# Moving the product dt·u to VectorE, and reordering loads and steps, in a fused two-layer graph kernel

## What is computed

```python
# layer 0
h  = relu(adj @ x @ gcn_w + gcn_b);  h = layernorm(h) * ln_g + ln_b
xc, z = split(h @ w_in)                        # 256 + 256 columns
u  = silu(causal_conv4(xc) + conv_b)
dbc = u @ w_xp                                 # 8 columns of dt, 16 of B, 16 of C
dt = softplus(dbc[:, :8] @ w_dt + b_dt)
state[t] = exp(dt[t] * A) * state[t-1] + dt[t] * B[t] * u[t]      # 256 x 16, along all 4096 rows
y  = (state[t] @ C[t] + u * D_skip) * silu(z)
x1 = layernorm(x + y @ w_out)
# layer 1
o1 = mlp3((2 + eps1) * (adj @ x1));  o2 = mlp3((2 + eps2) * (adj @ x2))
out = layernorm(x1 + concat(o1, o2) @ Wm.T + bm)
```

## Time and profile before

| | |
|---|---|
| median of 3 runs | 820.49 us (820.03 to 822.79) |
| the profiled execution | 821.7 us |
| its span, first to last instruction | 819.9 us |
| TensorE busy | 805.8 us (98%) |
| VectorE busy | 599.7 us (73%) |
| ScalarE busy | 377.9 us (46%) |
| GpSimd busy | 659.7 us (80%) |
| DMA | 227.6 MB, mean 278 GB/s |

### The profile page before, as it was taken

One profiled execution on the slowest core, in us unless ns is written; L12 is line 12 of the kernel. 1 busy time (PEld: TensorE's weight loads), 2 busy tenths in 40 slices (PEclk: granted clock), 3 DMA queues, 4 the chain that ended last, 5 costly groups with the idle time before them and its releaser, 6 DMA issues.

```text
span 819.9 us, 7302 instructions
## 1 busy us (share of the span) xinstructions
PE 805.8 (98%) x2078; PEld 365.8 (45%) x2078; DVE 599.7 (73%) x800; ACT 377.9 (46%) x615; POOL 659.7 (80%) x318
## 2 busy tenths in 40 slices
PE   8899999999999999999999999999999999999996
PEld 3344444444444444444444444444444454444453
DVE  0034898799868986898799879887988889882135
ACT  0154465357535653475347534652466445231234
POOL 2005999999999899899999999889998999970036
PEclk9999999999999999999999999999999999999999
DMA  8979767675766899899778976789867896887602
GB/s 336 385 270 368 267 242 250 231 251 201 271 202 201 333 349 355 343 352 361 245 249 320 379 278 213 254 291 384 295 235 272 327 329 245 297 306 261 254 26 78
DMA packets 63388, 227.59 MB, mean 278 GB/s; under 512 B 7394, under 2 KB 8052, under 8 KB 44916
## 3 DMA queue, kind: packets, MB, share of 16 engines
q1 hardware_dynamic: 24660, 156.33, 50.9%
q10 hardware_dynamic: 38688, 70.80, 26.4%
HBM read 224.48 MB, written 2.62 MB: 277 GB/s over the span
## 4 chain that ended last, share of the span: by engine, by line
PE 95%; DMA 4%; ACT 1%; DVE 0%; issue 0%; DVEq 0%
PE p_x L486 51%; PE p_x L509 16%; PE p_two L509 11%; DMA x_s<-x_tiles 3%; PE p_m L582 2%; PE p_dA L677 2%; PE p_m L598 2%; PE p_two L572 1%; PE p_m L565 1%; DMA ring<-adj_blocks 1%; PE p_m L602 1%; PE p_m L536 1%; PE p_m L542 1%; PE p_h L677 1%; PE p_m L594 1%; PE p_two L552 1%
## 5 line engine op out<-in xcount | busy, mean ns | idle before, releaser
L486 PE MATMUL p_x<-ring,x_s 128*128 128x512 f32 x1024 | 459.2, 597 | 4.2 <-DMA x_s<-x_tiles 4.2
L1125 POOL TENSOR_TENSOR y<-y,prod 128x1024 f32<-128x1024 f32 x127 | 299.4, 2357 | 26.6 <-DVE prod L942 25.9
L486 PEld LDWEIGHTS p_x<-ring,x_s 128*128 128x128 f32 x1024 | 193.8, 191 | 252.1 <-issue 242.5
L1116 POOL TENSOR_TENSOR bh<-spread,dtu 128x1024 f32<-128x1024 f32 x128 | 302.1, 2360 | 2.1 <-DMA spread<-bc_rows 2.0
L933 DVE TENSOR_TENSOR_SCAN p_h<-p_dA,state,bh 128x512 f32<-128x512 f32 x224 | 276.2, 1279 | 25.3 <-ACT p_dA L687 11.3
L687 ACT ACTIVATE p_dA<-dt,A 128x512 f32<-128x512 f32 x256 | 170.8, 686 | 113.0 <-DVE p_h L933 109.9
L942 DVE TENSOR_TENSOR prod<-p_h,spread_C 128x1024 f32<-128x1024 f32 x128 | 155.3, 1213 | 0.0
L509 PE MATMUL p_x<-ring,x 128*128 128x512 f32 x304 | 137.2, 593 | 0.0
L509 PE MATMUL p_two<-ring,x 128*128 128x512 f32 x208 | 94.5, 593 | 0.5 <-DVE dt L992 0.5
L509 PEld LDWEIGHTS p_x<-ring,x 128*128 128x128 f32 x304 | 57.4, 190 | 72.6 <-issue 72.6
L415 POOL TENSOR_SCALAR dtu<-prod,mv,rstd 128x128 f32<-128x128 f32 x26 | 20.3, 794 | 64.0 <-ACT rstd L920 64.0
(11 more groups left out here) (125 smaller groups left out, 579.9 us busy)
## 6 DMA issues: line engine op xcount, KB each, us to landing
ring<-adj_blocks SPq DMA_DIRECT2D x143, 1024.0 KB, 7.2
spread<-bc_rows ACTq DMA_DIRECT2D x128, 256.0 KB, 5.1
spread_C<-bc_rows ACTq DMA_DIRECT2D x128, 256.0 KB, 5.7
ring<-adj_blocks SPq DMA_DIRECT2D x8, 256.0 KB, 5.8
x_s<-x_tiles SPq DMA_DIRECT2D x8, 256.0 KB, 7.4
x_s<-x_tiles ACTq DMA_DIRECT2D x7, 256.0 KB, 7.5
out_tiles<-dtu SPq DMA_DIRECT2D x7, 256.0 KB, 2.0
pack<-pack_w ACTq DMA_DIRECT2D x1, 1026.5 KB, 11.2
```

The source lines that it names most:

```text
L486: return pe.matmul(bank[:, :], tiles[:, JT * m + jt, :], ring[:, i % RING, jt, :], start=opens, stop=closes)
L1116: pool.tensor_tensor(bh[:, i % 3, :, :], both(spread[:, i % SLOTS, :]), dtu[:, c % 2, :, :], ALU.mult).then_inc(s_bmul, 1)
L1125: pool.tensor_tensor(y[:, c % 2, :, :], y[:, c % 2, :, :], prod[:, i % 2, :, :], ALU.add).then_inc(s_acc, 1)
```

## The change

- "dt_sum" on VectorE writes max(v, 0) + ln(...) back into the banks (`s_dtsum`), ScalarE copies them to `dt_` (new step "dt_copy" at unit 11, ahead of "y_init", `s_dt`), VectorE multiplies the banks by u (new step "dtu" at unit 11, place 1, `s_dtu`, two instructions). The product on GpSimd is gone. TensorE's waits for the banks are on `s_dtu` in place of `s_dt`.
- In the fill, ScalarE takes softplus before it issues the first two broadcast rows of B.
- x1 is issued without a wait, x2 to x7 behind earlier landings than before, and the pack behind x7.
- The MLP steps of chunks 1 to 6 come half a unit later, the second of chunk 7 one unit sooner.
- The last "out" comes behind one block of `AFTER_BLOCKS`.
- VectorE no longer negates the means; ScalarE negates rstd. The state is not copied in the last chunk.

```diff
-        return [(c - 1, (24, 26, 28, 30))]
-    return [(6, (6, 9, 12, 15)), (7, (24, 26, 28, 30))]
+        return [(c - 1, (25, 27, 29, 31))]
+    return [(6, (6, 9, 12, 15)), (7, (22, 24, 26, 28))]
...
                         if unit > origin(chunk) and chunk + 1 < NC:
-                            pe.wait_ge(s_dt, G * (chunk + 1) + 1)
+                            pe.wait_ge(s_dtu, G * (chunk + 1) + 1)
...
                 elif name == "z":
-                    pe.wait_ge(s_dt, G * (n + 1))
+                    pe.wait_ge(s_dtu, G * (n + 1))
...
                     if n < 6:
-                        pe.wait_ge(s_dt, G * (n + 3))
+                        pe.wait_ge(s_dtu, G * (n + 3))
...
             block_part(AFTER_AT, 0, JT)
-            block_part(AFTER_AT + 1, 0, JT)
             step("out", NC - 1)
-            for i in range(AFTER_AT + 2, TAIL_AT):
+            for i in range(AFTER_AT + 1, TAIL_AT):
...
+                elif name == "dt_copy":
+                    for q, (g, bank) in enumerate(((1, p_two), (0, p_m))):
+                        act.wait_ge(s_dtsum, G * n + q + 1)
+                        act.activation(dt_[:, b, g, :], bank[:, :], ACT.Copy).then_inc(s_dt, 1)
...
+                    act.activation(nrstd[:, :], rstd[:, b, :], ACT.Copy, scale=-1.0).then_inc(s_rv, 1)
+                    act.wait_ge(s_rv, 3 * n + 3)
                     for t in range(JT):
-                        last = act.activation(shift[:, t:t + 1], nmean[:, t:t + 1], ACT.Copy, scale=rstd[:, b, t:t + 1])
+                        last = act.activation(shift[:, t:t + 1], mv[:, b, t, 0:1], ACT.Copy, scale=nrstd[:, t:t + 1])
...
                     put(o + 6, "softplus", c + 1)
+                    put(o + 7, "dt_copy", c + 1)
                     put(o + 7, "y_init", c + 1)
...
-                if k < 4:
-                    act.wait_ge(s_tile[(0, 0, 3, 7)[k]], 32 if k == 1 else 16)
-                else:
-                    act.wait_ge(*filled(k - 2))
+                if k == 2:
+                    act.wait_ge(s_tile[1], 32)
+                elif k in (3, 4):
+                    act.wait_ge(s_tile[3 * k - 7], 16)
+                elif k > 4:
+                    act.wait_ge(*filled(k - 3))
                 act.dma_start(x_s[:, JT * k:JT * (k + 1), :], x_d[k]).then_inc(s_xs[k], 16)
-                if k == 6:
-                    act.dma_start(pack[:, :], pack_d).then_inc(s_pack, 16)
+            act.dma_start(pack[:, :], pack_d).then_inc(s_pack, 16)
...
-                if name == "rows":
+                if name == "softplus":
                     for i in range(AHEAD):
                         spread_row(i)
...
-                dve.tensor_copy(state[:, unit, :], p_h[:, :, T - 1]).then_inc(s_state, 1)
+                if c < NC - 1:
+                    dve.tensor_copy(state[:, unit, :], p_h[:, :, T - 1]).then_inc(s_state, 1)
...
                     for g, bank in ((1, p_two), (0, p_m)):
-                        dve.scalar_tensor_tensor(out=dt_[:, b, g, :], in0=bank[:, :], scalar=0.0, in1=dt_[:, b, g, :],
-                                                 op0=ALU.max, op1=ALU.add).then_inc(s_dt, 1)
+                        dve.scalar_tensor_tensor(out=bank[:, :], in0=bank[:, :], scalar=0.0, in1=dt_[:, b, g, :],
+                                                 op0=ALU.max, op1=ALU.add).then_inc(s_dtsum, 1)
+                elif name == "dtu":
+
+                    dve.wait_ge(s_u, G * (n + 1))
+                    for q, (g, bank) in enumerate(((1, p_two), (0, p_m))):
+                        dve.wait_ge(s_dt, G * n + q + 1)
+                        dve.tensor_tensor(dtu[:, b, g, :], bank[:, :], u[:, g, :], ALU.mult).then_inc(s_dtu, 1)
...
                     put(o + 7, 0, "dt_sum", c + 1)
+                    put(o + 7, 1, "dtu", c + 1)
...
-                if name == "dtu":
-                    pool.wait_ge(s_dt, G * (n + 1))
-                    pool.wait_ge(s_u, G * (n + 1))
-                    pool.tensor_tensor(dtu[:, b, :, :], dt_[:, b, :, :], u[:, :, :], ALU.mult).then_inc(s_dtu, 1)
...
```

More of the change, by code:

```diff
@@ L297, in two_layer_graph_kernel @@
         rstd = sb("rstd", [P, 4, JT])
-        nmean = sb("nmean", [P, JT])
+        nrstd = sb("nrstd", [P, JT])
         shift = sb("shift", [P, JT])
@@ L365, in two_layer_graph_kernel @@
         s_dbcp, s_xpart, s_xsum, s_dbc = (sem(n) for n in ("s_dbcp", "s_xpart", "s_xsum", "s_dbc"))
[L366 to L370, removed]
+        s_dtp, s_abs, s_sp, s_dtsum, s_dt, s_dtu, s_yinit = (sem(n) for n in (
+            "s_dtp", "s_abs", "s_sp", "s_dtsum", "s_dt", "s_dtu", "s_yinit"))
+        s_yg, s_o, s_r, s_stats, s_rv, s_shift, s_x1 = (sem(n) for n in (
+            "s_yg", "s_o", "s_r", "s_stats", "s_rv", "s_shift", "s_x1"))
         s_mm2, s_mr2, s_res0, s_res1, s_two_add = (sem(n) for n in ("s_mm2", "s_mr2", "s_res0", "s_res1", "s_two_add"))
@@ L762, in step @@
                 elif name == "silu":
-                    wait(act, s_dtu, n)
+                    wait(act, s_dtu, G * n)
                     wait(act, s_yinit, G * n)
@@ L865, in _ @@
             take_x(0)
-            for name in ("gcn", "cen", "var", "in_x", "silu", "log_exp", "x_part", "rows", "softplus", "y_init"):
+            for name in ("gcn", "cen", "var", "in_x", "silu", "log_exp", "x_part", "rows", "softplus", "dt_copy", "y_init"):
                 step(name, 0)
@@ L928, in scans @@
                 wait(dve, s_cmul, i)
-                wait(dve, s_state, i)
+                wait(dve, s_state, min(i, S * (NC - 1)))
                 for g in range(G):
@@ L999, in step @@
                     statistics(r4, s_stats, n)
-                    aggregate(s_stats, b).then_inc(s_aggr, 1)
-                    dve.wait_ge(s_aggr, n + 1)
-                    dve.tensor_scalar(nmean[:, :], mv[:, b, :, 0], -1.0, None, ALU.mult).then_inc(s_stats, 1)
+                    aggregate(s_stats, b).then_inc(s_stats, 1)
                 elif name == "mlp3":
@@ L1051, in _ @@
             dve.wait_ge(s_two_add, 1)
-            for name in ("var", "taps0", "taps1", "x_sum", "dt_sum"):
+            for name in ("var", "taps0", "taps1", "x_sum", "dt_sum", "dtu"):
                 step(name, 0)
@@ L1076, in _ @@
             add_sum(SUM_OF[AFTER_AT])
-            add_sum(SUM_OF[AFTER_AT + 1])
             step("out", NC - 1)
-            for no in range(SUM_OF[AFTER_AT + 2], SUM_OF[TAIL_AT]):
+            for no in range(SUM_OF[AFTER_AT + 1], SUM_OF[TAIL_AT]):
                 add_sum(no)
@@ L1112, in times_B @@
                 if unit == 0:
-                    pool.wait_ge(s_dtu, c + 1)
+                    pool.wait_ge(s_dtu, G * (c + 1))
                 wait(pool, s_scan, G * (i - 2))
@@ L1128, in step @@
             def step(name, n):
-                b = n % 2
-                if name == "dtu":
-                    pool.wait_ge(s_dt, G * (n + 1))
-                    pool.wait_ge(s_u, G * (n + 1))
-                    pool.tensor_tensor(dtu[:, b, :, :], dt_[:, b, :, :], u[:, :, :], ALU.mult).then_inc(s_dtu, 1)
-                elif name == "gate_y":
+                if name == "gate_y":
                     pool.wait_ge(s_acc, S * (n + 1))
                     pool.wait_ge(s_gate, n + 1)
-                    pool.tensor_tensor(y[:, b, :, :], y[:, b, :, :], gate[:, :, :], ALU.mult).then_inc(s_yg, 1)
+                    pool.tensor_tensor(y[:, n % 2, :, :], y[:, n % 2, :, :], gate[:, :, :], ALU.mult).then_inc(s_yg, 1)
                 elif name == "resid":
@@ L1163, in _ @@
             pool.tensor_copy(wx3[:, :, ROW_B + S:ROW_B + 2 * S], w_xp[:, :, R + S:R + 2 * S]).then_inc(s_wx3, 1)
-            step("dtu", 0)
             for i in range(AHEAD):
@@ L1174, in _ @@
                         step("gate_y", c - 1)
-                    if c + 1 < NC and unit == origin(c) + 8:
-                        step("dtu", c + 1)
                     if i + AHEAD < S * NC:
```

4 lines of the change are left out of this document (2 added, 2 removed).

## The result

| | before | changed |
|---|---|---|
| median, timed together | 820.64 us (819.10 to 823.83, 6 runs) | 823.49 us (822.72 to 825.55, 6 runs) |
| the profiled execution | 821.7 us | 822.72 us |
| its span | 819.9 us | 820.9 us |
| mean granted clock of TensorE in it | 0.998 | 0.995 |

A forecast was written before the change was run, and what follows sets the result against it. TensorE, busy 98% of the span, was taken as the bound, so only its gaps could pay. Ramp -2.5 us and chunk 2's stall +2.5 us summed to 0.0: 820.5 us on the median, range 817.7 to 823.6.

The forecast's parts named there:

- ramp: At the start, x tiles issued ahead of weights close two DMA gaps: -2.5 us, bounds -0.8 and -3.7.
- line 536: The matmul after the ramp that first needs the pack; a sign of the forecast was its start near 37.3 us.
- (b): Rival: scan work falls behind TensorE through ScalarE's queue and VectorE's unit 11, stalling chunks 3 and 5; 824.3 us, chance 0.10.
- (d): Rival: at the ramp the first gap closes but block 7 lands where x7 did; ramp 0, 823.0 us, chance 0.10.
- The stall: In chunk 2, p_two's opening waits for VectorE's product with u: +2.5 us, bounds +1.3 and +3.8.
- Block 1: At the ramp, with x1 there, its first load starts near 11.1 us, 1.49 us sooner.
- The wait of block 2: At the ramp, x tiles moved forward delay this weight block on full DMAs, so it binds near 15.3 us.
- Block 7: At the ramp, the last to land, at 32.8 us, first load 32.85; wrong if landing before 31 or after 34.
- The pack: The 1 MB transfer issued after x7 lands at about 33 to 34 us, hidden with over 2 us of cover.
- Softplus first: In the fill, ScalarE's softplus starts about 4 us sooner, ahead of B's broadcasts; worth 0 us.
- (a): Rival: the ramp gives much (-3.7 us) and chunk 2's stall is short (+1.3 us); 817.5 us, chance 0.17.
- (c): Rival: the pack lands late, at 38 us, and holds line 536, costing 1.6 us; 822.1 us, chance 0.05.

The follow-up runs named there:

- e12: The kernel before the change, with no edit, traced a second time; 819.51 us in one execution.
- e2: The kernel before with only the dt change (sums in the banks, ScalarE's copy, VectorE's product with u); 825.20 us against 820.67, ratio 1.0057.
- e3: The kernel before with all edits of the change except the x order with the pack and the dt change; 820.44 us against 820.67, ratio 1.0001.
- e7: The kernel before with only a longer TensorE wait at chunk 2's opening of p_two, for ScalarE's second y_init; 821.03 us in one execution.
- e8: The kernel before with the dt change and softplus ahead of B's broadcasts in the fill; 823.42 us against 820.22, ratio 1.0043.
- e1: The kernel before with only the order of the x tiles and the pack changed; 819.13 us against 820.67, ratio 0.9984.
- e11: The changed kernel timed again, with no edit; 823.78 us against 821.21 for the kernel before, ratio 1.0020.
- e5: The changed kernel with VectorE's products with u directly behind the sums; 822.05 us against 820.22 for the kernel before, ratio 1.0014.

## Why the prediction's range held and its sum did not, step by step

**The accounts.** By the starts of weight loads, from an ordinary trace of before (e12, span 817.7) to the changed one (820.9): ramp (line 536 from 37.59 to 36.81) -0.8, gap in chunk 2 +2.4, half pace behind it +1.6; sum +3.2, which is also the difference of the spans. The forecast had -2.5 + 2.5. The range held the time by luck: its upper end comes from the forecast's outer bounds taken together (-0.8 and +3.8) and from rivals (b) and (d). The stall was not near its bound, neither rival took place, and a second price on the stall was no part of the range.

**Two terms failed.** First, the size of the ramp's gain: -2.5 was read from one execution, whose x7 took 10.97 us to land where others took 9.1. Against that execution the gain is even more than forecast (39.78 to 36.81, -3.0 us). But line 536 comes at 37.3 to 37.6 in four of the six traces with the old order (e2, e3, e7, e12; mean 37.5) and at 39.8 and 42.0 in the other two (before, e8); in the eight with the new order it comes at 36.8 to 38.0 (mean 37.2). So the new order gains 0.2 us over an ordinary ramp, 1.4 us over the mean of all six, and the timing of e1 says 1.5: nearly all of it is late executions that no longer come. The working had a sign of it: that execution, 821.7 us, lay 1.2 us above the median that the sum was then applied to. Second, the clock. The prediction read from the earlier trace rows that loads at half pace are 0.86 us apart, but took the stall to cost its length alone. The lower level behind it cost 1.6 us in the changed trace, 1.7 us in e2 and e11 and 3.0 us in e8; e5 and e7, with steps of 3.30 and 3.24 us, show none in their traces. At the ramp, a step of 2.88 us is followed by full pace and one of 3.77 us (e8) by half pace. For the slow loads before 10.2 us in the earlier trace rows the lower clock is inferred from their pace alone: the granted clock reads 1.00 from 8 to 12 us there, while in chunk 2 pace and granted clock fall together.

The Trainium skill, "TensorE: Matmul & The Clock Gate", section "Part 1: The HAM clock gate", has the lower clock as the default of an engine that was idle, given up once the engine is busy again. The traces of this case agree: in the changed kernel, e2, e8 and e11 a step of 3.9 us is followed by loads 0.85 us apart. It was the rule that spoke against this change, and the prediction did not weigh it; by the changed trace it would have added +1.6 us.

**The stall was right.** Place, mechanism, order on VectorE and size: 3.91 us instead of "about 4", +2.4 us against +2.5. Against the lower bound (+1.3 us, the product directly behind the sum), e5 shows that even there the step is 3.30 us: +1.8, because both sums and ScalarE's copy go first.

**The DMAs at the ramp.** Block 1 at 11.06 was right (forecast 11.1). The wait of block 2 until 15.20 has the time of the forecast (15.3) but not its reason: block 2, issued at 5.38, had landed at 14.8, and the wait was for its x tiles, issued at 7.08 behind an earlier landing and there after 8.08 us. Block 7 landed at 30.6, not at 32.8, and below the 31 that the prediction itself named as a sign of being wrong: it was not "the last" at all. Its first load, at 32.04 instead of 32.85, comes where TensorE's own queue of blocks lets it, so that this part of the working failed and its time came near by luck. Line 536 came at 36.81 (37.3). (The "seven blocks" that bring block 7 to 31.6 are six; the time is that of six.)

The pack landed at 33.3, 2.7 us behind block 7. The Trainium skill, "DMA: Bandwidth & Descriptors", section "Queues, rings and completion order", has each DMA engine take turns between queues by whole packets. The trace after agrees: from 22.4 to 30.6 us the queues moved nearly the same number, 387 packets (q1) and 409 (q10, the last x tiles among them). But the 387 carried 2.21 MB and the 409 only 1.17 MB. What failed is the prediction's own step from there, that the two are alike in packet size and so would finish together.

**Smaller steps.** GpSimd's busy time fell by 18.0 us (19 forecast). The MLPs, "out" and the state copies at 0 us: e3 agrees. Softplus first at 0 us was right alone; beside the dt change it may hide 1.2 us (e2 against e8), which is not shown. VectorE's busy time was to rise by 7 us and fell by 0.5, because the negated means that went had cost 8.0 us, for a reason given below.

**The rivals.** (a) had both terms at their better ends; neither was there. (b), scan work falling behind, has its right sign and nearly its time (824.3), but not its mechanism: chunks 3 and 5 have no new gap, in the changed kernel or in e2; what came near it was e2's gap in chunk 0 and e5's in chunk 3. (c) no: the pack landed at 33.3, 3.5 us ahead of line 536. (d) no: block 7 waits for no x tile. What took place was none of them: the forecast's own stall with a second price on it, and a ramp that gave less.

**What stays open.** Why x7 lands 9.1 us after its issue in one execution and 11 or 12 us in the next (before, e8), in the old order, was not tried. Nor was what sets how long the lower clock lasts (1.6 to 3.0 us lost behind equal steps). That the 2 to 3 us between the two groups of executions in e5 and e11 are the clock's is argued from the granted clock of each execution, since only one of each was traced.

## What to carry to other kernels

Before work goes in front of the release of a bank, look which instruction opens that bank next and how much queue lies between; here the one opening without cover cost the whole slowdown, and moving one block ahead of it gave 5.3 us back. Price a stall of TensorE by its length and by the lower clock that may follow it, and look for both in the starts of the weight loads, where steps twice the regular one point to the clock and the granted clock of the stretch confirms it. Take the size of a transfer's gap from more than one execution: a median is not moved by closing a gap that only a late execution has.

## What the runs showed of the hardware that was not expected

The negation of the means, 128x4 elements, took VectorE 1005 ns on average in the kernel before (group of the trace of before; the columns are busy us in all, mean ns, idle before). The products of 128x512 that the change adds take 0.68 us each (the first of their two groups after). Eight small instructions cost 8.0 us and sixteen large ones 10.9; with 16 state copies of 0.15 us gone too, VectorE's busy time hardly moved.

```profile
L1002 DVE TENSOR_SCALAR nmean<-mv 128x4 f32<-128x4 f32 x8 | 8.0, 1005 | 0.3
```
```profile
L1007 DVE TENSOR_TENSOR dtu<-p_two,u 128x512 f32<-128x512 f32 x8 | 5.5, 681 | 0.1
```

The mean hides two cases. Of the eight negations, the two for which GpSimd is idle take 0.17 us. Each of the other six starts while GpSimd is in an instruction of 2.4 us and ends 0.01 to 0.03 us behind that instruction's end, whether that takes 0.21 us or 2.37 us. The longest of them (timelines of VectorE and of GpSimd, before):

```profile
502.45 2.37 DVE L1002 TENSOR_SCALAR nmean<-mv 128x4 f32<-128x4 f32 x1
```
```profile
502.42 2.37 POOL L1116 TENSOR_TENSOR bh<-spread,dtu 128x1024 f32<-128x1024 f32 x1
```

So this small instruction waits for GpSimd without any semaphore between them, and its time is what is left of GpSimd's. The products of the change, with one operand in a bank, run beside GpSimd at 0.68 us without such a wait.

And the granted clock: behind a step of 3.91 us it was at the lower level for a stretch that cost 1.6 us in one trace and 3.0 us in another, once beginning at once and once (e11) four loads later, and in 3 of 12 executions of e11 its mean shows no fall at all.
